# Softmax sums out of the values' own products in the second and third attention: row masks, one reciprocal and a shuffle on VectorE in place of separate products on TensorE

## The reference

```python
# L=1: 128 queries, keys = 128 context + 128 latents (256), 16 heads of 16
attn = jnp.where(full_mask[:, None, None, :], jnp.einsum('bkhd,bnhd->bhkn', q, kmat) / DH, -jnp.inf)
attn = jax.nn.softmax(attn, axis=-1)
out = jnp.einsum('bhkn,bnhd->bkhd', attn, v).reshape(b, k_len, H)
# L=2: 128 queries, 128 keys, 16 heads of 16, the same form; then for both:
out = out @ out_w + out_b + residual     # norm and an MLP of 1024 behind it
```

## Time and profile before

| | us |
|---|---|
| median of 3 runs | 1096.55 (1096.37 to 1098.66) |
| the profiled execution | 1094.25 |
| its span, the time that the profile covers | 1092.1 |
| TensorE busy with products / loading weights | 955.9 (88%) / 608.2 (56%) |
| VectorE busy | 541.6 (50%) |
| ScalarE busy | 484.3 (44%) |
| GpSimd busy | 268.1 (25%) |

### The profile page before, as it was taken

How to read it: one execution, slowest core, us unless ns; L and a number is a source line. 1 busy time by engine, 2 the same in 40 slices (tenths; PEclk the granted TensorE clock), 3 DMA queues, 4 the chain that set the end, 5 groups by cost and what they waited for, 6 DMA issues and landing times.

```text
span 1092.1 us, 21492 instructions
## 1 busy us (share of the span) xinstructions
PE 955.9 (88%) x8592; PEld 608.2 (56%) x8592; DVE 541.6 (50%) x1012; ACT 484.3 (44%) x937; POOL 268.1 (25%) x389
## 2 busy tenths in 40 slices
PE   7799999999899989999999998999899999976672
PEld 6466664666456664666547664556646665444430
DVE  2444555445645455445554555355554555443440
ACT  1424454364543545345543545445553455423233
POOL 0230220243111521223211421116112332113203
PEclk9899999999999999999999999999999999988886
DMA  9300220001310202002300113102120022002001
GB/s 372 134 2 1 78 98 27 18 5 80 106 35 1 79 18 104 25 2 82 106 19 18 37 48 107 35 2 80 50 72 24 2 83 97 27 9 77 5 2 38
DMA packets 29057, 60.14 MB, mean 55 GB/s; under 512 B 9376, under 2 KB 21024, under 8 KB 24096
## 3 DMA queue, kind: packets, MB, share of 16 engines
q1 hardware_dynamic: 28960, 58.77, 14.7%
HBM read 53.52 MB, written 5.24 MB: 54 GB/s over the span
## 4 chain that ended last, share of the span: by engine, by line
PE 72%; DVE 12%; issue 9%; ACT 4%; POOL 1%; DMA 1%; DVEq 0%; ACTq 0%; POOLq 0%; SPq 0%
DVE nm L1393 6%; PE PV L712 6%; PE GP L966 6%; PE GP L574 6%; PE GP L975 5%; PE GP L576 5%; PE SC L695 4%; PE GP L950 4%; PE SC L884 3%; PE GP L759 3%; PE SC L781 3%; PE GP L798 2%; PE GP L581 2%; PE PV L897 2%; PE MX L628 2%
## 5 line engine op out<-in xcount | busy, mean ns | idle before, releaser
L1393 DVE TENSOR_REDUCE nm<-MX 128x2 bf16<-128x512 f32 (+1 forms) x352 | 227.0, 689 | 169.7 <-PE MX L634 79.6
L1705 POOL TENSOR_TENSOR Psum<-Pr 128x512 f32<-128x512 f32 x56 | 71.3, 1274 | 255.7 <-ACT Pr L1188 255.7
L1190 ACT ACTIVATE Pr<-SC,bcol 128x512 f32<-128x512 f32 x128 | 81.0, 684 | 108.6 <-PE SC L781 108.6
L574 PE MATMUL GP<-zP,W 128*128 128x128 f32 x512 | 103.5, 284 | 7.1 <-DMA W<-w 7.1
L576 PE MATMUL GP<-uP,W 128*128 128x128 f32 x512 | 99.7, 277 | 0.0
L1188 ACT ACTIVATE Pr<-SC 128x512 f32<-128x512 f32 x128 | 69.6, 599 | 57.1 <-PE SC L695 57.1
L1215 ACT ACTIVATE Pr<-SC,bcol 128x512 f32<-128x512 f32 x96 | 60.8, 685 | 63.5 <-PE SC L884 63.5
L574 PEld LDWEIGHTS GP<-zP,W 128*128 128x128 f32 x512 | 78.9, 193 | 17.1 <-issue 15.3
L576 PEld LDWEIGHTS GP<-uP,W 128*128 128x128 f32 x512 | 78.5, 194 | 0.0
L1679 POOL TENSOR_TENSOR stat<-stat,half 128x1 f32<-128x1 f32 x24 | 13.6, 565 | 259.3 <-DVE stat L1560 163.1
L712 PE MATMUL PV<-Pr,V 128*64 128x256 f32 x512 | 69.4, 392 | 0.8
(11 more groups left out here) (188 smaller groups left out, 1708.4 us busy)
## 6 DMA issues: line engine op xcount, KB each, us to landing
WA<-w1a SPq DMA_DIRECT2D x8, 1024.0 KB, 4.8
WB<-w1b SPq DMA_DIRECT2D x8, 1024.0 KB, 7.3
WA<-w2a SPq DMA_DIRECT2D x8, 1024.0 KB, 5.0
WB<-w2b SPq DMA_DIRECT2D x8, 1024.0 KB, 7.1
W<-w SPq DMA_DIRECT2D x6, 1024.0 KB, 10.0
scratch<-U SPq DMA_DIRECT2D x16, 256.0 KB, 2.0
C<-scratch SPq DMA_DIRECT2D x96, 32.0 KB
zP<-z_in SPq DMA_DIRECT2D x8, 128.0 KB, 4.5
```

Source lines behind the costliest of these rows:

```text
L574: pe.matmul(dst, W0[:, piece, 2 * s, at:at + P], zP[:, s * P:s * P + P], start=True, stop=False)
L1190: act.activation(Pr[:, (n + j) % 4, :], SC[j], ACT.Exp, bias=bcol[:, 3 + k % 2:4 + k % 2], scale=8.0 ** -0.5).then_inc(p_ready, 1)
L1393: dve.tensor_reduce(dst, MX[(n + i) % 2][:].rearrange("p (a k) -> p a k", a=a), AX_X, ALU.max, negate=True).then_inc(mx_done, 1)
L1705: pool.tensor_tensor(Psum[:, c % 4, :].rearrange("p (a l) -> p a l", l=D), two[:, :, 0:D], two[:, :, D:2 * D], ALU.add)\
```

## The change

The weights' 16 free columns beside each head's 16 values are set to one instead of zero (the memsets of `V1` and `V2`; the values are written over the rest as before). A values' product then gives in one go, for r = 0, values in rows 0 to 15 of a strip and their sums in rows 16 to 31, and for r = 1 the other way round. The two groups no longer share columns: r = 0 goes to columns 0 to 127 of the bank and r = 1 to columns 128 to 255. The separate sums' products and `ones2` are gone; `pv` issues 4 products for each r in place of 8.

VectorE's `quotient` now takes the two apart with two row masks, `low` (1 in rows 0 to 15 of each strip) and `high` (1 in rows 16 to 31), two new columns of `hmask`: Ax = even x low + odd x high, and den = even x high + odd x low. Then one reciprocal of den, a shuffle in each strip that swaps its two halves of 16 rows, so that a reciprocal comes to the rows of its values, and the product. Of the seven instructions the first, the third and the last are not chained.

```diff
-V_STEPS = 2 + 4 + 4
+V_STEPS = 2 + 4 * 4 + 4
...
-        hmask = sb("hmask", [P, 4 + 4 + 2 + 128])
+        hmask = sb("hmask", [P, 4 + 4 + 2 + 128 + 2])
+        low, high = hmask[:, 138:139], hmask[:, 139:140]
...
-        ones2 = sb("ones2", [P, 2, 32])
+        swapped = sb("swapped", [P, P])
...
-                        for at, weights in ((0, lambda t: V(2 * c + r, t, kc)), (P, lambda t: ones2[:, r, :])):
-                            for t in range(4):
-                                mm = pe.matmul(bank[32 * t:32 * t + 32, at:at + P], weights(t),
-                                               Pr[:, (n + r) % 4, t * P:t * P + P], start=(at == kc == r == 0),
-                                               stop=(kc == halves - 1 and r == 1), skip_group_check=True)
+                        for t in range(4):
+                            mm = pe.matmul(bank[32 * t:32 * t + 32, r * P:r * P + P], V(2 * c + r, t, kc),
+                                           Pr[:, (n + r) % 4, t * P:t * P + P], start=(kc == r == 0),
+                                           stop=(kc == halves - 1), skip_group_check=True)
                         mm.then_inc(pv_done, 1)
...
-                chain.step(dve.reciprocal(den, bank[:, P:2 * P]))
-                dve.tensor_tensor(Ax[:, m, :], bank[:, 0:P], den, ALU.mult).then_inc(s_Ax, 1)
+                even, odd = bank[:, 0:P], bank[:, P:2 * P]
+                dve.tensor_scalar(Ax[:, m, :], even, low, None, ALU.mult)
+                chain.step(dve.tensor_scalar(den, even, high, None, ALU.mult))
+                dve.scalar_tensor_tensor(out=Ax[:, m, :], in0=odd, scalar=high, in1=Ax[:, m, :], op0=ALU.mult,
+                                         op1=ALU.add)
+                chain.step(dve.scalar_tensor_tensor(out=den, in0=odd, scalar=low, in1=den, op0=ALU.mult,
+                                                    op1=ALU.add))
+                chain.step(dve.reciprocal(den, den))
+                chain.step(dve.stream_shuffle(swapped[:], den, [(r + 16) % 32 for r in range(32)]))
+                dve.tensor_tensor(Ax[:, m, :], Ax[:, m, :], swapped[:], ALU.mult).then_inc(s_Ax, 1)
...
-            dve.memset(V1[:], 0.0)
+            dve.memset(V1[:], 1.0)
             dve.memset(V3[:], 1.0)
-            dve.memset(V2[:], 0.0).then_inc(const_v, 1)
+            dve.memset(V2[:], 1.0).then_inc(const_v, 1)
...
-            pool.memset(ones2[:], 0.0)
             pool.memset(sums2[:], 0.0).then_inc(const_p, 1)
...
-                pool.memset(ones2[:, i, 16 * i:16 * i + 16], 1.0)
...
-                            p[:, None] // 32 % 2 == np.arange(2)[None], *spread],
+                            p[:, None] // 32 % 2 == np.arange(2)[None], *spread,
+                            p[:, None] // 16 % 2 == np.arange(2)[None]],
```

## The result

The changed kernel takes 1148.92 us (median of 4 runs, 1145.64 to 1149.79) against 1096.74 before (four runs, the three of the table and one more): a ratio of 1.0469, 95% interval 1.0449 to 1.0490. It is slower, as forecast, but by 52 us and not by 29, and it lies outside the range. The profiled execution has a span of 1148.0 us, 55.9 more than before. TensorE has 768 instructions fewer and is busy 12.3 us longer (968.2 against 955.9): the first sign that some of the others take longer than before.

What follows compares the result with a forecast made beforehand. TensorE's in-order queue, 72% of the chain of waits, was taken to set the pace. Longer quotients outweighed the saved products: 26.0 us in seven batches plus 3.8 in the last gave 29.8, forecast 1125 us, range 1109 to 1141.

Steps and rivals of the forecast that it cites:

- The work taken off: TensorE loses 96 groups of products with `ones` weights, 0.22 us each: 21.1 us leave its queue.
- The sum: All batches' lateness: 26.0 us in batches 0 to 6 plus 3.8 in the last, 29.8; as formula 31X - 21.4.
- X: What one quotient costs more on VectorE: 1.65 us, bounds 1.3 and 2.3.
- L=1: Second attention, batches 0 to 6: TensorE waits at the maxima product and `slots_out`, late by 1.58 us a batch.
- L=2, the waits: Third attention, batches 0 to 6: late shift copy and second quotient delay TensorE by 2.13 us a batch.
- The idle time ahead of L613, L689 and L958: Sign: TensorE's idle before L=1's second maxima product, L=2's scores and `slots_out` grows by some 25 us in all.
- The clock falls: Rival: TensorE idles longer, one more slice a batch at 0.8 clock adds 27 us, about 1152 us; 4%.
- The last batch: No other work between its stages: 0.95 us late in L=1 and 2.86 in L=2, together 3.8 us.

Runs made afterwards that it cites:

- the wait filled: Changed kernel plus eight unused 128x128 products behind the last values' product of L=2, inside TensorE's wait for the shift copy: 1130.12 us.
- the exchange of the copy alone: Changed kernel with the shift copy for the next batch's L=0 put ahead of the first quotient in L=2: 1145.86 us.
- the two kernels whose last batch is kept busy: Unused products in last-batch waits: changed kernel, L=2's waits filled too, 1126.03 us; kernel before, shift copy ahead of L=2's first quotient, 1088.94 us.
- the shorter quotient: Changed kernel without the sums' masks and the shuffle, so values are not divided by their own sums: 1101.98 us.

## Why the prediction was wrong, step by step

- **The work taken off.** Right: the groups with `ones` are gone, and of their 21.1 us 9 to 10 pay with the quotient unchanged. The sum's formula gives at X = 0 a gain of 2.89 us a batch; 1.5 were measured, so it holds only near break-even (0.69 against a measured 0.65) and above.
- **X.** Right: 1.62 against 1.65. Masked operations 0.34 to 0.35, shuffle 0.29, loading its permutation 0.01, the overlap of 0.08 as read. The row was the one to go by. The prediction set against it a rule of the Trainium skill (VectorE: DVE Perf Modes, "The DRAIN you can't avoid"), by which X would have been 1.81, but it left out half of it: the same section says that a next operation that is not held starts earlier, and the overlap of 0.08 agrees with that.
- **L=1.** Right: forecast 1.58, measured 1.71 at the transposition of xb and 1.74 with this attention changed alone. Both waits are where they were put, 1.26 us at the maxima product and 1.43 at `slots_out`.
- **L=2, the waits.** Right: forecast 2.13, measured 2.3 with the wait filled (130.6 less the 128.3 of L=1 alone) and 1.9 to 2.3 with L=2 alone where the clock stays up. The idle time ahead of L613, L689 and L958, by which I wanted to see the lateness, grew by 40 us and not by the 25 that I gave: the shorter `pv` calls bring TensorE to each wait earlier, and that adds to the idle time but not to the lateness.
- **The clock.** This is the step that failed. Every term of the sum priced TensorE's products at full clock, and the rival *The clock falls* had 4%, though its 1152 us and its one more dip a batch are nearly what came. That its total is so near is partly luck: it priced a dip at 3.9 us, from the clock of a whole slice in the last batch, and 17.0 us in seven batches is 2.4 each; the last batch and the waits made up the rest. The prediction looked for no place where the clock would fall. What counted was where the idle time stood: the wait for the copy in L=2, with 1.51 of 3.70 us busy around it. The longer quotient alone brings the fall in six of seven batches and the shorter `pv` calls alone in none; both together bring it in all seven, for 6.8 us each. With the wait filled it is gone, and with it 17.0 us.
- **The last batch.** Forecast 3.8, measured 9.3, and 6.8 with L=2 filled; but with the exchange of the copy alone it is 6.2, so some 3 us of this is what the last batch moves by itself. The idle time put down to `Ax` grew by 4.9 us (7.0 against 2.1). Between the two kernels whose last batch is kept busy it is 137.2 - 131.2 = 6.0 us, at mean clocks of 0.83 and 0.86, and the idle time for `Ax` differs by 3.0 (5.0 against 2.0). So the waits are about what was forecast, and a good part of the rest is the clock again, as the shorter quotient's last batch says too. An exact split isn't shown.
- **The sum.** At full clock 29.8 was forecast. The two kept-busy kernels differ by 1126.0 - 1088.9 = 37.1 us, of which the copy's order makes 7 x 0.4 = 2.8: 34 us. The waits of the seven batches were right within about 2 us (26.0 forecast, 28.1 measured). The rest of the miss is 17.0 us in them, which is the clock, and 5.5 in the last (9.3 less 3.8), which is the clock only in part as far as is shown.

## What to carry to other kernels

Work that is taken off the busiest engine pays only where that engine's own columns end the wait; find the slack of each product by its neighbours before counting its columns. Where a change makes TensorE idle at a place where it has just become less busy, price the products behind it at half clock too, and ask this of the place and not of a slice of the whole span. A wait that can't be removed may be filled with unused products into a free bank: here that was worth 19 us in the slower kernel, which stays 3% slower than the kernel before, and 3 us in the last batch of the faster one. Needed work in the same place does it too (16 us), where it brings no new wait behind it.

## What the runs showed that I had not expected

- In the seven batches of the changed kernel the clock fell with no single idle time of TensorE ahead of it longer than 2.19 us.
- With the same 2.19 us of wait for the copy the clock fell in five of seven batches with L=2 changed alone and in all seven with both, and the batches of the kernel with the long quotient alone alternate (132.3 and 134.1 us).
- VectorE's half of the change alone takes as long as the whole of it, 1148.3 and 1148.9 us: it has longer waits and less time at half clock.
- At break-even of the waits (X = 0.65) the last batch is still 6.9 us longer.
